# Routing scratch moved into PSUM, y stores threaded between the loads of expert rows, and a new order on every engine

## What is computed

```python
x = x + attn(layernorm(x))      # 16 heads of 8; q, k l2-normed per head; no softmax: (q k^T / n**sigmoid(m)) v, then Wo
h = layernorm(x)
logits = h @ router_w.T                       # 16 experts, top 1
s = sigmoid(top logit), 0 for all other experts
routed = down[e](up * silu(gate)), gate, up = split((h * s) @ gate_up[e])
shared = (silu(h @ shared_gate_w.T) * (h @ shared_up_w.T)) @ shared_down_w.T
x = x + shared + routed
```

## Time and profile before

| | |
|---|---|
| time, median of 3 runs | 239.5 us (238.86 to 240.54) |
| span of the profiled execution, first to last instruction | 238.7 us |
| median of the runs less that span | 0.8 us |
| PE busy | 198.3 us (83%) |
| DVE busy | 153.4 us (64%) |
| ACT busy | 107.4 us (45%) |
| POOL busy | 95.2 us (40%) |
| moved by DMA | 22.57 MB, 95 GB/s on average |

### The profile page before, as it was taken

The page is one execution under the profiler, slowest core; times in us unless marked ns, Lnnn a source line. Parts: engine busy times, 40 slices in busy tenths (PEclk is TensorE's granted clock), DMA queues, the critical chain, the costliest instruction groups (busy, mean ns, idle before and its releaser), DMA issues.

```text
span 238.7 us, 3742 instructions
## 1 busy us (share of the span) xinstructions
PE 198.3 (83%) x1126; PEld 160.1 (67%) x1126; DVE 153.4 (64%) x480; ACT 107.4 (45%) x236; POOL 95.2 (40%) x122
## 2 busy tenths in 40 slices
PE   0975589989899798569999979999999999999300
PEld 0422446757668666469888868999998888888200
DVE  4499986999999965655866677754551444525411
ACT  3324546483868965561224655765543232232000
POOL 5002412566678778667500000000000666756650
PEclk9999999999999799756999999999999999999955
DMA  6999960000001001001135445722233131211631
GB/s 167 350 396 142 306 269 3 1 22 24 19 30 44 22 22 47 22 22 46 36 67 112 104 106 109 186 59 76 71 105 91 35 93 46 76 49 50 211 91 55
DMA packets 22279, 22.57 MB, mean 95 GB/s; under 512 B 2803, under 2 KB 17397, under 8 KB 22005
## 3 DMA queue, kind: packets, MB, share of 16 engines
q1 hardware_dynamic: 19056, 16.75, 25.6%
q0 software_dynamic: 2048, 4.21, 6.4%
q10 hardware_dynamic: 1156, 1.39, 1.7%
HBM read 13.93 MB, written 8.41 MB: 94 GB/s over the span
## 4 chain that ended last, share of the span: by engine, by line
PE 27%; DMA 25%; DVE 23%; issue 8%; ACT 7%; SPq 5%; POOL 3%; POOLq 0%; DVEq 0%; ACTq 0%
DMA h_rows<-y_slots,y_row 16%; PE quad_banks L1221 6%; DVE qkv L731 5%; PE bank L1240 4%; SPq L245 4%; DVE st L694 3%; DMA xres<-L_attn_x 3%; ACT h_rows L447 3%; DMA x_slots<-h_rows,pos 3%; DVE ss L739 2%; POOL h_rows L405 2%; PE bank L1229 2%; DVE rn L744 2%; DVE far L765 2%; PE bank L1198 2%
## 5 line engine op out<-in xcount | busy, mean ns | idle before, releaser
L405 POOL DMA_INDIRECT h_rows<-y_slots,y_row x32 | 31.4, 982 | 82.0 <-DMA y_slots<-yg 65.5
L821 DVE TENSOR_TENSOR s_act<-quad_banks,sg_act 128x512 f32<-128x512 f32 x32 | 22.1, 691 | 33.2 <-ACT sg_act L491 31.8
L491 ACT ACTIVATE sg_act<-quad_banks 128x512 f32<-128x512 f32 x32 | 19.1, 597 | 51.3 <-PE quad_banks L1178 51.3
L332 POOL DMA_INDIRECT x_slots<-h_rows,pos x32 | 31.6, 986 | 17.4 <-DVE pos L782 8.2
L1198 PEld LDWEIGHTS bank<-sdT,s_act 128*128 128x128 f32 x256 | 33.4, 196 | 2.8 <-DVE s_act L821 0.7
L1198 PE MATMUL bank<-sdT,s_act 128*128 128x128 f32 x256 | 34.7, 281 | 0.5 <-DVE s_act L821 0.5
L1094 PE MATMUL quad_banks<-w_c,xT 128*128 128x384 f32 x64 | 26.3, 541 | 6.0 <-DVE qkv L731 5.5
L308 POOL TENSOR_TENSOR qkv<-qkv,rn 128x512 f32<-128x512 f32 x16 | 17.0, 1078 | 32.7 <-DVE rn L744 32.6
L1221 PE MATMUL quad_banks<-w_gu,xgT 128*128 x96 | 22.9, 381 | 0.0
L1094 PEld LDWEIGHTS quad_banks<-w_c,xT 128*128 128x128 f32 x64 | 12.0, 207 | 16.2 <-issue 6.2
L694 DVE BATCH_NORM_STATS2 st<-xres 128x6 f32<-128x128 f32 x64 | 13.7, 276 | 8.6 <-ACT xres L441 5.3
(11 more groups left out here) (144 smaller groups left out, 375.5 us busy)
## 6 DMA issues: line engine op xcount, KB each, us to landing
xg<-x_slots SPq DMA_DIRECT2D x48, 64.5 KB, 1.9
y_slots<-yg SPq DMA_DIRECT2D x12, 256.0 KB, 2.3
xT<-x_t SPq DMA_DIRECT2D x8, 256.0 KB, 6.7
xres<-L_attn_x SPq DMA_DIRECT2D x8, 256.0 KB, 6.9
w_gu<-gate_up SPq DMA_DIRECT2D x1, 2048.0 KB, 14.2
x_slots<-zeros SPq DMA_DIRECT2D x1, 1032.0 KB, 16.2
w_dn<-down SPq DMA_DIRECT2D x1, 1024.0 KB, 16.1
out<-xres SPq DMA_DIRECT2D x4, 256.0 KB, 2.3
```

What stands on the lines that cost most here:

```text
L332: g.indirect_dma_start(out=x_slots, out_offset=bass.IndirectOffsetOnAxis(ap=pos[:, t:t + 1], axis=0), in_=h_rows[:, t, :], in_offset=None) ...
L405: g.indirect_dma_start(out=h_rows[:, t, 0:D], out_offset=None, in_=y_slots, in_offset=bass.IndirectOffsetOnAxis(ap=y_row[:, t:t + 1], axis ...
L821: v.tensor_tensor(s_act[:, n % 2], pair[:, 2 * (n % 2) + 1], sg_act[:, n % 2], ALU.mult).then_inc(s_act_rdy, 1)
```

## The change

Four things, and nothing of what is computed.

**Scratch in PSUM.** `far`, `offs` and `rank` are no longer SBUF tiles but columns of the bank that holds the chunk's logits:

```diff
+        def far_of(c):
+            return log_bank(c)[:, 192:192 + Q * E].rearrange("p (t e) -> p t e", e=E)
+
+        def offs_of(c):
+            return log_bank(c)[:, 256:256 + Q * E].rearrange("p (e t) -> p e t", t=Q)
+
+        def rank_of(c):
+            return log_bank(c)[:, 320:320 + Q]
...
-                link(v.tensor_tensor(far[:], logits, top.unsqueeze(2).broadcast_to([P, Q, E]), ALU.is_lt))
-                link(v.scalar_tensor_tensor(out=far[:], in0=far[:], scalar=FAR, in1=place_of[:], op0=ALU.mult,
+                link(v.tensor_tensor(far, logits, top.unsqueeze(2).broadcast_to([P, Q, E]), ALU.is_lt))
+                link(v.scalar_tensor_tensor(out=far, in0=far, scalar=FAR, in1=place_of[:], op0=ALU.mult,
                                             op1=ALU.add))
...
-                link(v.tensor_tensor(offs[:], offs[:], hot[:, c], ALU.mult))
+                link(v.tensor_tensor(offs, offs, hot[:, c], ALU.mult))
```

**`h_scales`.** The one instruction with two SBUF inputs becomes four with one input and a scalar column:

```diff
-                v.scalar_tensor_tensor(out=nm2[:, t], in0=mv2[:, t, 0], scalar=-1.0, in1=rs2[:, t], op0=ALU.mult,
-                                       op1=ALU.mult).then_inc(rstd2, 1)
+                for n in tiles(c):
+                    last = v.tensor_scalar(nm2[:, n:n + 1], mv2[:, n, 0:1], rs2[:, n:n + 1], -1.0, ALU.mult, ALU.mult)
+                last.then_inc(rstd2, 1)
```

**SyncE.** After `load(8)` the queue goes on with store(0), store(1), load(9), store(2), load(10), load(11), and then stores 3 to 11:

```diff
-            for g in range(NG):
-                load(g)
-            for g in range(NG):
-                store(g)
+            load(0)
...
+            load(8)
+            store(0)
+            store(1)
+            load(9)
+            store(2)
+            load(10)
+            load(11)
+            store(3)
...
```

**All orders.** Every engine's list of calls is laid out anew (on TensorE some calls get a wait more, or lose one that another wait implies). The parts that matter for the text below:

```diff
 VectorE, the start
+            bias_rows()
+            scale_mask()
+            x_scales(0)
             x_stats(1)
-            x_scales(0)
+            take(0, 0)
             x_stats(2)
...
 VectorE, round the norms of chunk 7
             head_sums(7)
-            x1_stats(5)
-            place(3)
             act_shared(0)
+            choose(3)
+            h_scales(4)
             inv_norms(7)
+            place(3)
+            x1_stats(5)
+            act_shared(1)
+            mask_vk(3)
             choose(4)
...
 TensorE, the end of routing
             turn_h(6, after=(hT_sb, 6))
+            down_shared(0, after=(x1_rdy, 8))
             route(6, after=(pos_rdy, 5))
+            gate_up_shared(4, after=(s_act_rdy, 3))
+            count_before(6)
             turn_h(7, after=(hT_sb, 7))
-            count_before(6)
-            down_shared(0, after=(x1_rdy, 8))
+            down_shared(1)
             route(7, after=(pos_rdy, 6))
-            gate_up_shared(4, after=(s_act_rdy, 3))
+            gate_up_shared(5, after=(s_act_rdy, 4))
             count_before(7)
```

More of the change, by code:

```diff
@@ L388, in _ @@
             count(6)
-            hT_lo(7)
             scatter(24)
@@ L1332, in _ @@
             gate_up_shared(9, after=(s_act_rdy, 8))
-            turn_rows(0, after=(pos_rdy, 7))
-            gate_up_shared(10, after=(s_act_rdy, 9))
             down_shared(8, after=(y_free, 2))
+            turn_rows(0)
+            gate_up_experts(0, after=(s_act_rdy, 9))
             turn_rows(1, after=(gT_sb, 1))
-            down_shared(9)
-            gate_up_experts(0, after=(s_act_rdy, 11))
             turn_rows(2, after=(gT_sb, 2))
             gate_up_experts(1, after=(s_act_rdy, 10))
+            turn_act(0)
@@ L1341, in _ @@
             turn_rows(3, after=(gT_sb, 3))
-            down_shared(10)
             gate_up_experts(2, after=(e_act_rdy, 1))
-            turn_act(0, after=(y_free, 1))
+            down_experts(0, after=(table_rdy, 1))
+            turn_act(1, after=(aT_sb, 1))
             gate_up_experts(3, after=(e_act_rdy, 2))
-            turn_act(1, after=(aT_sb, 1))
-            down_experts(0, after=(table_rdy, 1))
+            gate_up_shared(10, after=(e_act_rdy, 3))
             turn_rows(4, after=(gT_sb, 4))
+            down_experts(1, after=(yg_rdy, 1))
@@ L1364, in _ @@
+            turn_rows(9, after=(gT_sb, 9))
+            turn_act(6, after=(aT_sb, 6))
             gate_up_experts(8, after=(e_act_rdy, 7))
-            turn_act(6, after=(aT_sb, 6))
-            down_experts(4, after=(yg_rdy, 4))
-            turn_rows(9, after=(gT_sb, 9))
-            gate_up_shared(11, after=(e_act_rdy, 8))
-            down_experts(5, after=(yg_rdy, 5))
+            down_experts(6, after=(yg_rdy, 6))
+            turn_act(7, after=(aT_sb, 7))
             turn_rows(10, after=(gT_sb, 10))
-            turn_act(7, after=(aT_sb, 7))
```

511 lines of the change are left out of this document (263 added, 248 removed).

## The result

The changed kernel takes 222.53 us (median of 4 runs, 222.22 to 225.01), the kernel before on the same chip 240.02 (238.86 to 242.48): ratio 0.930, 95% interval 0.924 to 0.936. Predicted were 225.0, range 216.5 to 232.0. The profiled execution took 222.22 us with a span of 220.2.

What follows compares the result with a forecast made beforehand. The prediction took three pieces in series to bound the kernel, with the gathers at the end. From a span of 238.7 it took 9 (front), 5.5 (experts) and 0 (way back): 224.2, plus 0.8 gives 225.0 us, range 216.5 to 232.

Steps and rivals of the forecast that it cites:

- Three pieces: Span in series: 121.4 us to the first expert-row load, 59.1 to the last expert product, 58.2 of way back.
- Way back, 0: Gathers after the last expert product: unchanged at 58.2 us, if the shared expert ends in time (cover 5.4 less about 1.5).
- Expert piece, 5.5: First expert-row load to last expert product: 7.7 us less TensorE work, part lost in gaps; gain 5.5, bounds 2 to 7.7.
- the cost of the stores between the loads: SyncE's queue: load(9) behind two stores brings group 9's rows late; with y_rows on VectorE, 1.5 us of gap.
- Front, 9 of a sum of 12: Up to the first expert-row load: four terms sum to 12.0 us, cut to 9 for GpSimd's floor; bounds 3 to 14.
- (1) Stretches, 6.5: VectorE instructions stretched beside GpSimd in the front: 10.0 us removed, less 2 for added instructions and 1.5 for new meetings.
- (2): Front, VectorE: bias_rows and scale_mask moved into the 3.04 us wait for x, gaining 1.5 us.
- (3): Front, VectorE: place(3) and x1_stats(5) behind inv_norms(7), so chunk 7's v and q reach GpSimd 2.2 us sooner; gain 2.
- (4): End of routing: shared products moved into TensorE's waits, four hT_lo out of GpSimd's scatters; gain 2 us, between 0 and 5.
- The floor: GpSimd's work from the first scatter, 56 us plus waits, would put the first expert-row load at 112 to 115.
- Rival D: All works and the clock stays up: front gains 14, experts 7.7, giving 217.8 us; chance 0.15.
- Rival C: nm2 in its new form still waits for GpSimd in the front: its 3.1 us stays, giving 228; chance 0.07.

Runs made afterwards that it cites:

- loads_first: Changed kernel with SyncE's queue as before, all twelve loads of expert rows and then all twelve stores: 221.96 us, ratio 0.930.
- late_fill: Changed kernel with gate_up_shared(4) and (5) moved on TensorE from beside route(6) and route(7) to behind count_before(7): 230.17 us, ratio 0.964.
- ring4_both_old_nm_fill: Changed kernel with four gather semaphores, single nm2 instruction, eight unread TensorE products, four scatter semaphores: four runs 225.0 to 225.7 us, two 218.7 and 220.4.
- inv7_back: Changed kernel with inv_norms(7) on VectorE moved back behind place(3) and x1_stats(5), as in the kernel before: 229.63 us, ratio 0.962.

## Why the prediction was right, and where its steps were not

**Three pieces.** Right; it carried the forecast. The expert piece kept its length under either front, though with the old front the times show only part of its gain.

**Way back, 0.** Right (58.5), though with 55.7 to 58.5 from one execution to another the agreement to 0.3 is partly luck. The cover held: the last add still waits for a gather, 4.20 us where 5.68 stood. What I had not seen is that this piece was for sale: a deeper ring takes 4.3 to 5.0 off it.

**Expert piece, 5.5.** 4.6 measured. TensorE's work in it shrank by 7.1 (busy 57.5 to 50.4 us), close to the 7.7 of the text, and its gaps grew by 2.5. The late rows are real (6.3 us of VectorE's waits against 4.7). The step that failed is the cost of the stores between the loads, part of the 1.5 of gap: `loads_first` shows none on balance.

**Front, 9 of a sum of 12; 14.1 measured.** The sum without the haircut for GpSimd's floor was nearer. By terms:
- (1) Stretches, 6.5. With the old order 5.0, right in kind. In the new order scratch in PSUM gives some 3.3 of time for 5.5 of stretches gone, and `nm2` loses 1.5 to 3.2. The sum took each stretch as its own excess over the median; what a stretch costs depends on what waits behind it. And it took `nm2`'s stretches from the old order, where the new one had already removed them. The three extra instructions were booked at 0.25 a chunk and cost 0.42.
- (2) `bias_rows` in the wait for x, 1.5: `inv_norms(0)` came 2.0 sooner (21.5 to 19.5). `take(0, 0)` moved up there as well, and no run separates the two.
- (3) `inv_norms(7)` two calls earlier, 2: undoing it in the new order cost 7.5. This is the mis-sized term. I priced the 2.2 us of work that stood ahead, not the clock behind it. In the old order `v_by_k(7)` (85.0) had no gap ahead of it, so 7.5 is its price among the other moves, not its share of the 14.1.
- (4) End of routing, 2 of 0 to 5: `late_fill` bears out 2.4 of it up to the last `pos`, but 0.4 up to the last scatter.
- The floor: the first scatter came at 44.4, 5.1 sooner, as forecast, and the last one ended at 105.7, 61 us later, where the sum had 56 and the waits on top. The estimate of 112 to 115 for the load took 8.2 us of waits for `pos` as before, and that was the wrong part; they fell to 2.1. With that the floor was close: SyncE waited only 0.4 us more for the last scatter's landing once the table was there (2.3 before), so the two limits of the front now stand nearly together.

What (3), (4) and the haircut have in common: I read the clock off one window, 100 to 110 us, and treated it as a local price. The runs show it as an amplifier of some gaps on TensorE, and not of all. Rival D had this ("the clock stays up, front 14") and was given 0.15; its front is what came, without its experts. Rival C fell (no `tensor_scalar` of `h_scales` was blocked), though the `nm2` edit was indeed worth less than nothing, by count and not by waiting. The Trainium skill ("SBUF — State Buffer", Who interferes with whom) also says that who issues first, not the kind of instruction, decides who waits; by its record the 1.80 us `nm2` began 0.51 before `hT_lo`, inside a scatter's 0.96, and was the one that waited. So the runs bear out the meeting; whether the scatter's end or something the records don't show gave GpSimd the first turn stays open.

## What to carry to other kernels

Before pricing an order, find each stretch in which TensorE's granted clock is below full and the gap just ahead of it; a move that closes the gap can be worth the half-speed stretch too, and one that opens it can cost that much, as long as no other engine was behind anyway (`late_fill`'s 2.4 us were 0.4 at the last scatter). Edits against the same stall don't add: test each in the final order, for one of them (here the four `tensor_scalar`) may by then be pure cost. And where a ring of transfers ends the chain, try its depth first.

## What the runs showed of the hardware

- Gaps of 1.88 (kernel before), 2.30 (`late_fill`), 2.61 (`ring4_both_old_nm_fill`) and 3.12 us (`inv7_back`) on TensorE in its busy routing stage were followed by 7 to 14 us at half clock. A gap of 1.38 us (changed kernel, 86.3 to 87.7) was not, while two of 0.72 and 0.76 close together (kernel before) came ahead of 3.4 us of it. `inv7_back` was 7.5 us longer than the changed kernel; the profiled execution of `ring4_both_old_nm_fill` was 7.0 longer than that of the kernel without its change (225.12 against 218.13), with a stretch of 5.3 us in it as well.
- The same instructions in the same order met either level from one execution to the next (1.00 or 0.56 from 25 to 30 us, with TensorE idle some 3 of the 5 us ahead in both), and the executions with the dip had their first load some 3 us later (110.0 and 110.4 against 107.2). That this kernel's spread of about 1% comes from there is likely, but not shown.
- A VectorE instruction of one column with a second SBUF input lasted 5.50 us beside four GpSimd instructions of 1.27 us in a row: it waited out the run, not one instruction. So did a `tensor_scalar` (int32, 128x16) with a single SBUF input, 2.47 us where it takes 0.17.
- An indirect gather of 128 rows was issued every 1.25 us when four might be in flight. With two the landings made it 1.45 to 1.55, by execution.
